# Constants of a delta-rule attention stage: loaded in the stage before, first group summed on VectorE, gate parameters made in the inverse stage

## The chip, the cores and the metric

The kernel runs as one program on one core of a Trainium2 chip. The metric is the time of one execution on the device, in microseconds (us). A line of the profile such as L1421 is that line of the kernel's source. Engines are named PE (TensorE, the matrix products; PEld is its weight load), DVE (VectorE), ACT (ScalarE), POOL (GpSimd) and SP (SyncE, which here issues nearly all transfers). A q behind a name is that engine's instruction queue.

## What is computed

Two transformer layers over 16 sequences of 256 tokens and 128 channels, in float32, each part followed by a residual sum and a layer norm:

```python
x = layernorm(x + L0_attn(x))        # RWKV-like attention with time mixing
x = layernorm(x + L0_ffn(x))         # 8 experts, the best two of each token, relu
x = layernorm(x + L1_attn(x))        # delta rule in chunks of 32 tokens, gate
x = layernorm(x + L1_ffn(x))         # 8 experts, the best one of each token, gelu
```

The change lies in and around the third. Cut to what matters:

```python
q, k, v = silu(conv4(x @ Wq)), silu(conv4(x @ Wk)), silu(conv4(x @ Wv))
beta = sigmoid(x @ Wb)
q, k = l2norm(q), l2norm(k)
A = where(i > j, -(k * beta) @ k.T, 0)      # 32 x 32 for each chunk and head
T = inverse of (I - A), row by row
u, w = T @ (v * beta), T @ (k * beta)
# chunk by chunk: o = q @ S + (q @ k.T, masked) @ (u - w @ S);  S += k.T @ (u - w @ S)
short, long = fir3(v), fir63(v)
logits = (gelu([x, stats(short, long, o, v)] @ gW1 + gb1) @ gW2 + gb2) / exp(log_temp)
floor = 0.05 * sigmoid(floor_param)
p = softmax(logits) * (1 - sum(floor)) + floor
out = p0*short + p1*long + p2*o + p3*v + sigmoid(conv_res_logit)*short + alpha*(x @ Wid)
out = rmsnorm(out) * o_norm_w @ Wo
```

## The kernel before

**Stages.** `block_program` (L2674) builds five stages one after another: the first attention, the experts of two choices (`expert_stage` with tag "b"), `delta_stage` (L2581), `gate_stage` (L1727) and the experts of one choice (tag "d"). `stage` puts an all-engine barrier, the clearing of the stage's semaphores and a second barrier (L2687, L2689) behind each. `delta_stage` is two blocks: `delta_project` (L1227) and `delta_invert` (L1615). Inside a block each engine runs its own program in the order in which it is written; semaphores (`wait_ge`, `then_inc`) are all that orders one engine against another.

**Experts.** Tiles of 128 token rows go through two products, eight tiles deep: SP loads tile j + 8 when the result of tile j is made (`s_y`, L1042, L1043). POOL scatters the results into the rows of `chosen`.

**Projection.** 8 groups of 512 tokens (two sequences). SP loads three parts of a group's rows (L1301: the residual rows and the two chosen expert results), for groups 0 and 1 at once, and then seven tables (L1308). PE, ACT and DVE each begin with `wait_ge(s_w, 112)`, a wait for all seven. POOL sums the parts (`row_sum`, L1412, L1414); DVE takes mean and variance (`row_stats`, L1550, L1553); ACT makes the reciprocal deviation (L1459, L1463); POOL normalises four tiles (`row_norm`, L1421); PE transposes them (L1394 for group 0, L1345 later); ACT copies them to c_xT (L1469); PE projects and convolves (L1350, L1362, L1366). DVE makes the weights by tap c_wc (L1568) ahead of the first `row_stats`. In the loop PE projects group n + 1 while DVE and ACT finish group n.

**Inverse.** PE transposes the chunk matrices A (L1654), ACT copies them (L1687), DVE inverts them row by row (L1712, L1719) while PE computes the long FIR (L1667) from the table keep_toe and ACT copies that out (L1690). Then PE transposes back (L1677) and ACT copies (L1695). SP only stores the FIR rows (L1641).

**Gate.** 8 groups again. SP loads eye32 (L1890), sixteen more tables (L1897), and then for each group the branches (L1877), the rows (L1880) and, from the state, the delta output (L1888). The opening is written out by hand: w_and_u products of groups 0 and 1 (L1942), additions (L1973), transitions (L1957), the transpose of g_wox (L2067), hidden products (L1997), two small products (L2073, L2074), carried products (L1986), then the transposes of the statistics (L2010). ACT makes three parameters (L2338 to L2341), DVE nine small operations (L2422 to L2431), and then the statistics of group 0 (L2445 to L2451), whose squares are ACT's (L2276). From L2524 on runs the loop over groups.

## Time and profile before

| | |
|---|---|
| median of three runs | 1115.13 us (1114.96 to 1118.66) |
| the profiled execution | 1115.36 us, its span 1113.6 us |
| PE busy | 916.2 us, 82% of the span |
| DVE, ACT, POOL busy | 67%, 50%, 41% |
| mean granted clock of PE | 0.89 |
| HBM traffic | 42.69 MB read, 27.51 MB written, 63 GB/s over the span |

The table is one profiled execution, all times in us from the start of the span. The experts of two choices end at about 516, the projection runs from 519 to 667, the inverse to 731, the gate stage from 732.5 to 997, the last experts to the end.
### The profile page before, as it was taken

The numbers are of one execution on the slowest core, as the hardware profiler recorded it, in microseconds if no ns is written. First come the engines' busy times: TensorE is split into PE (matmuls) and PEld (weight loads), VectorE is DVE, ScalarE is ACT, GpSimd is POOL, SyncE is SP. The second block draws the span as 40 slices with busy tenths as digits, with TensorE's granted clock in tenths as the row PEclk, the third lists the DMA queues.
The fourth block names the chain that finished last, engine by engine and source line by source line (L and its number), as shares of the span: only waits on it lengthen the run. The fifth ranks groups of instructions, "written<-read, shape, count | busy, mean of one in ns | idle before, by whom it ended". The sixth has DMA issues, their size and how long they took to land. (4 is left out here: it accounts for less than half of the span.)

```text
span 1113.6 us, 34222 instructions
## 1 busy us (share of the span) xinstructions
PE 916.2 (82%) x12773; PEld 647.2 (58%) x12774; DVE 742.9 (67%) x2240; ACT 556.6 (50%) x1120; POOL 459.1 (41%) x585
## 2 busy tenths in 40 slices
PE   7899999999943999994789969468999987419995
PEld 3466666666622988993344437365565553218884
DVE  3568888898544555552588888903698788745664
ACT  1456667666411554552566753143555554316663
POOL 1001234553373444443477620021135444655776
PEclk7699999999965999997799989766899997758998
DMA  3011112217012222123334231132112234011120
GB/s 90 20 40 49 31 50 59 69 50 227 27 45 65 63 56 60 54 60 101 88 89 87 40 106 57 77 100 64 40 55 65 60 111 139 10 51 49 52 57 17
DMA packets 122117, 73.15 MB, mean 66 GB/s; under 512 B 63363, under 2 KB 108521, under 8 KB 121600
## 3 DMA queue, kind: packets, MB, share of 16 engines
q1 hardware_dynamic: 114176, 58.06, 19.3%
q0 software_dynamic: 6656, 12.70, 3.5%
q8 instruction: 94, 1.54, 0.6%
q10 hardware_dynamic: 1152, 0.53, 0.2%
q14 instruction: 39, 0.32, 0.1%
HBM read 42.69 MB, written 27.51 MB: 63 GB/s over the span
## 5 line engine op out<-in xcount | busy, mean ns | idle before, releaser
L1150 ACT ACTIVATE bx_h<-bx_up,bx_cur 128x128 f32<-128x128 f32 x288 | 82.3, 368 | 98.5 <-PE bx_up L1121 93.8
L593 POOL DMA_INDIRECT regions_b<-a_xo,a_seat x64 | 66.1, 1032 | 128.7 <-DVE a_seat L891 111.7
L1079 POOL DMA_INDIRECT chosen_b<-bx_ys,bx_to x72 | 74.0, 1028 | 92.1 <-DVE bx_ys L1193 69.4
L701 ACT ACTIVATE a_at<-a_scores 128x1024 f32<-128x1024 f32 x64 | 65.7, 1026 | 58.2 <-PE a_scores L463 57.7
L1121 PE MATMUL bx_up<-bx_xT,bx_cur 128*128 128x128 f32 x576 | 82.4, 287 | 2.1 <-DVE bx_cur L1166 0.6
L1103 PE MATMUL bx_down<-bk_w,bx_h 128*128 x576 | 82.1, 285 | 0.3 <-ACT bx_h L1150 0.3
L1121 PEld LDWEIGHTS bx_up<-bx_xT,bx_cur 128*128 128x128 f32 x576 | 71.1, 194 | 11.3 <-DVE bx_cur L1166 5.5
L1103 PEld LDWEIGHTS bx_down<-bk_w,bx_h 128*128 128x128 f32 x576 | 69.7, 191 | 3.5 <-issue 0.5
L1350 PE MATMUL c_bank<-c_xT,c_wc 128*128 128x512 f32 x128 | 62.5, 633 | 7.2 <-DVE keep_attn L1542 6.4
L1166 DVE TENSOR_SCALAR bx_cur<-bk_w 128x516 f32 x72 | 31.3, 434 | 52.9 <-issue 50.4
L458 PE MATMUL a_scores<-a_rk,a_kx 32*128 32x128 f32 (+3 forms) x1024 | 57.7, 290 | 4.6 <-DVE a_kx L769 3.7
L458 PEld LDWEIGHTS a_scores<-a_rk,a_kx 32*128 32x128 f32 x1024 | 43.4, 187 | 29.9 <-issue 14.2
L463 PE MATMUL a_scores<-a_rk,a_kx 32*128 32x32 f32 (+3 forms) x1024 | 53.3, 273 | 0.0
L1421 POOL TENSOR_SCALAR c_xn<-c_part,c_mv,c_rsv 128x128 f32<-128x128 f32 x32 | 35.1, 1107 | 37.0 <-ACT c_rsv L1463 37.0
L2170 POOL COPY g_kak<-keep_k 128x512 f32<-128x512 f32 x16 | 9.8, 616 | 97.3 <-POOLq L2689 67.0
L1350 PEld LDWEIGHTS c_bank<-c_xT,c_wc 128*128 128x128 f32 x128 | 25.6, 204 | 41.5 <-issue 32.6
L1121 PE MATMUL dx_up<-dx_xT,dx_cur 128*128 128x128 f32 x320 | 47.7, 294 | 1.0 <-ACT dx_cur L1139 0.5
L1079 POOL DMA_INDIRECT out_rows<-dx_ys,dx_to x40 | 43.5, 1087 | 8.1 <-issue 8.1
L1150 ACT ACTIVATE dx_h<-dx_up,dx_cur 128x128 f32<-128x128 f32 x160 | 45.1, 363 | 3.2 <-PE dx_up L1121 3.2
L1139 ACT ACTIVATE dx_cur<-space 128x516 f32 x40 | 25.3, 633 | 42.4 <-ACT dx_h L1150 26.6
L1103 PE MATMUL dx_down<-space,dx_h 128*128 x320 | 46.1, 287 | 0.3 <-ACT dx_h L1150 0.3
L1121 PEld LDWEIGHTS dx_up<-dx_xT,dx_cur 128*128 128x128 f32 x320 | 40.4, 198 | 8.7 <-ACT dx_cur L1139 7.4
(440 smaller groups left out, 2462.7 us busy)
## 6 DMA issues: line engine op xcount, KB each, us to landing
bx_xs<-regions_b SPq DMA_DIRECT2D x72, 65.0 KB, 1.8
bk_w<-in_b_w SPq DMA_DIRECT2D x16, 256.0 KB, 6.1
c_part<-chosen_b SPq DMA_DIRECT2D x16, 256.0 KB, 3.8
space<-in_d_w SPq DMA_DIRECT2D x16, 256.0 KB, 5.8
dx_xs<-regions_d SPq DMA_DIRECT2D x40, 65.0 KB, 1.8
a_xp<-in_a_xT SPq DMA_DIRECT2D x8, 256.0 KB, 3.4
a_xr<-in_x SPq DMA_DIRECT2D x8, 256.0 KB
lion_values<-a_vt SPq DMA_DIRECT2D x8, 256.0 KB, 2.7
```

The lines of the kernel that those rows point to most:

```text
L458: mm(S4[:, g, o:o + P - 32 * q], kx[rows, 0, 4 * t + q].rearrange("p h j -> p (h j)"), rk[b][rows, 0, t * P + 32 * q:(t + 1) * P], start=T ...
L463: i = mm(S4[:, g, o + P - 32 * q:o + P + 32], kx[rows, 1, 4 * t + q].rearrange("p h j -> p (h j)"), rk[b][rows, 2, t * P:t * P + 32 * q + 32],
L593: nc.gpsimd.indirect_dma_start(route["regions"], bass.IndirectOffsetOnAxis(ap=seat[b][:, k, t:t + 1], axis=0), xo[b][k][:, t, :], None).th ...
L701: op(at[m % 2][:], S4[:, :, 0:320].rearrange("p g (q k) -> p g q k", q=2)[:, :, :, 0:P], ACT.Copy).then_inc(s_ata, 1)
L1079: nc.gpsimd.indirect_dma_start(dest, bass.IndirectOffsetOnAxis(ap=to[u][:, 0:1], axis=0), ys[u][:], None, bounds_check=dest.shape[0] - 1, ...
L1103: i = mm(BY[u % 2][:, 0:P], h[u % 2][:, f, :], w2[:, bass.ds(e, 1), f, :].rearrange("p e c -> p (e c)"), start=(f == 0), stop=(f == FC - 1))
L1121: i = mm(BU[u % 2][:, f * P:(f + 1) * P], cur[u % 2][:, f * P:(f + 1) * P], xT[u % 2][:], start=True, stop=True)
L1139: op(cur[u % 2][:], w1[:, bass.ds(e, 1), :].rearrange("p e c -> p (e c)"), ACT.Copy).then_inc(s_cur, 1)
L1150: i = op(h[u % 2][:, f, :], BU[u % 2][:, f * P:(f + 1) * P], act_fn, bias=cur[u % 2][:, FC * P + f:FC * P + f + 1])
L1166: v.tensor_scalar(cur[u % 2][:], w1[:, bass.ds(e, 1), :].rearrange("p e c -> p (e c)"), 1.0, None, ALU.mult).then_inc(s_cur, 1)
L1350: i = mm(B[1 + k].rearrange("p (s t) -> p s t", s=GSEQ), wc[:, k, j, :], xT[:, :, j:SEQ + j], start=(j == 0), stop=(j == 3))
L1421: nc.gpsimd.tensor_scalar(xn[:, t, :], part[b][0][:, t, :], mv[:, t, 0:1], rsv[:, t:t + 1], ALU.subtract, ALU.mult).then_inc(s_xn, 1)
```

## The change

Seven tables of the projection are allocated outside the stages and loaded by SP in the experts of two choices, behind the first eight row loads. In the projection the waits for them are gone. The third part of group 0 is issued by ACT, which then loads its table of functions at once. DVE sums and normalises group 0; POOL starts with the sums of group 1 when DVE has made those of group 0. All seventeen tables of the gate stage are loaded by SP at the start of the inverse block, ACT makes the three parameters there after its FIR copies, and in the gate stage DVE makes its parameters ahead of the first transitions, PE transposes g_wox before the first additions, and the hidden products of group 0 stand ahead of the transitions and of the additions of group 1. Some scratch rows of the stage's end lie in g_hid.

```diff
...
             return sem(f"{tag}_{name}")
...
-        s_c = s("identity_in")
...
             sp.dma_start(ident[:], consts[:, columns]).then_inc(s_c, 16)
             for u in range(U):
                 load(u, u)
+            for dst, src in early:
+                sp.dma_start(dst, src).then_inc(s_early, 16)
...
             rounds(sp, body)
+            if early:
+                sp.wait_ge(s_early, 16 * len(early))
...
+def project_tables(nc, ctx, w, consts):
...
+    con = sb("con", [P, columns.stop - columns.start])
+    t = {"C": {k: con[:, a:b] for k, (a, b) in where.items()},
+         "wqkv": sb("wqkv", [P, 3, P]), "wb": sb("wb", [P, P]), "taps": sb("taps", [P, 4]),
+         "tapr": sb("tapr", [P, 2, 4, P]), "fir": sb("fir", [P, 3]), "ident": sb("ident", [P, P])}
+    loads = [(con[:], consts[:, columns]), (t["wqkv"][:], w["wqkv"]), (t["wb"][:], w["wb"]), (t["taps"][:], w["taps"]),
+             (t["ident"][:], consts[:, constant_columns("ident", "ident")[1]]),
+             (t["tapr"][:].rearrange("p k j c -> p (k j c)"), w["tapr"].broadcast_to([P, 8 * P])), (t["fir"][:], w["firs"])]
+    return t, loads
...
+def delta_project(nc, sem, keep, x_parts, xT_out, v_rows, s_rows, tables, w):
...
-            def load(n, b):
-                for k in range(3):
+            def load(n, b, parts=(0, 1, 2)):
+                for k in parts:
                     sp.dma_start(part[b][k][:], one(part_tiles[k], n)).then_inc(s_x[b], 16)
-            load(0, 0)
+            load(0, 0, parts=(0, 1))
             load(1, 1)
-            for dst, src in [(con[:], consts[:, columns]), (wqkv[:], w["wqkv"]), (wb[:], w["wb"]), (taps[:], w["taps"]),
-                             (keep["ident"][:], consts[:, constant_columns("ident", "ident")[1]]),
-                             (tapr[:].rearrange("p k j c -> p (k j c)"), w["tapr"].broadcast_to([P, 8 * P])), (fir[:], w["firs"])]:
-                sp.dma_start(dst, src).then_inc(s_w, 16)
...
         @block.tensor
         def _(pe):
             mm = nc.tensor.matmul
-            pe.wait_ge(s_w, 112)
...
-            row_sum(0, 0, 0)
-            row_norm(0, 0, first=True)
+            pool.wait_ge(s_zs, 2)
             row_sum(1, 1, 0)
             row_norm(1, 1)
             row_sum(2, 0, 1)
...
-            act.wait_ge(s_w, 112)
+            act.dma_start(part[0][2][:], one(part_tiles[2], 0)).then_inc(s_x[0], 16)
+            nc.scalar.preload_act_table_set("natural_log_exp_and_others")
             act.wait_ge(s_set, 5)
...
-            nc.scalar.preload_act_table_set("natural_log_exp_and_others")
             row_logarithm(0)
...
-            dve.wait_ge(s_w, 112)
             dve.wait_ge(s_set, 5)
...
                 i = v.tensor_tensor(wc[:, k], tapr[:, k], wqkv[:, k, :].unsqueeze(1).broadcast_to([P, 4, P]), ALU.mult)
             i.then_inc(s_wc, 1)
             own.restart(dve)
+            x, y0, y1 = part[0]
+            dve.wait_ge(s_x[0], 48)
+            v.tensor_tensor(x[:], x[:], y0[:], ALU.add).then_inc(s_zs, 1)
+            dve.wait_ge(s_zs, 1)
+            v.tensor_tensor(x[:], x[:], y1[:], ALU.add).then_inc(s_zs, 1)
             row_stats(0, 0, first=True)
+            dve.wait_ge(s_rv, 1)
+            for t in range(GT):
+                v.tensor_scalar(xn[:, t, :], x[:, t, :], mv[:, t, 0:1], rsv[:, t:t + 1], ALU.subtract, ALU.mult).then_inc(s_xn, 1)
             row_stats(1, 1)
             convolve_values(0)
...
         def _(sp):
+            for dst, src in loads:
+                sp.dma_start(dst, src).then_inc(s_later, 16)
             sp.wait_ge(s_fc, 8)
...
                    ACT.Copy).then_inc(s_fc, 1)
+            act.wait_ge(s_later, 16 * len(loads))
+            op(later["floor"][:], later["fpar"][:], ACT.Sigmoid)
+            op(later["res"][:], later["crl"][:], ACT.Sigmoid)
+            nc.scalar.preload_act_table_set("natural_log_exp_and_others")
+            op(later["itc"][:], later["temp"][:], ACT.Exp, scale=-1.0)
...
+    loads = [(con[:], consts[:, columns]), (t["eye32"][:], consts[:, constant_columns("eye32", "eye32")[1]]),
+             (t["fpar"][:], w["floor"]), (t["crl"][:], w["crl"]), (t["temp"][:], w["temp"]),
+             (t["g1"][:], w["g1"]), (t["g1s"][:], w["g1s"]), (t["gb1"][:], w["gb1"]), (t["gw2"][:], w["gw2"]),
+             (t["wid"][:], w["wid"]), (t["wox"][:, 0:P], w["wo"]), (t["onw"][:], w["onw"]), (t["gbias"][:], w["gbias"]),
+             (t["alpha"][:], bc(w["alpha"], 4)), (t["gb"][:], bc(route["gate_b"], NE)),
+             (t["ident_gate"][:, P:P + NE], route["gate_w"]),
+             (t["ident_gate"][:, 0:P], consts[:, constant_columns("ident", "ident")[1]])]
+    return t, loads
...
         cnt = sb("cnt", [1, NE])
-        over = sb("over", [1, NE, TOK // P])
+        rows = lambda a, b, n: hid[0:1].rearrange("p j t -> p (j t)")[:, a:b].rearrange("p (k m) -> p k m", k=n)
+        over, le, lt, ef = rows(0, 256, NE), rows(256, 576, NT), rows(576, 896, NT), rows(896, 976, 2)
         base = [sb(f"base{i}", [1, 4 + NE]) for i in range(2)]
         skipped = sb("skipped", [1, NE])
-        le = sb("le", [1, NT, NE])
-        lt = sb("lt", [1, NT, NE])
-        ef = sb("ef", [1, 2, NT])
...
-            sp.dma_start(eye32[:], eye).then_inc(s_in, 16)
-            loads = [(con[:], consts[:, columns]), (g1[:], w["g1"]), (g1s[:], w["g1s"]), (gb1[:], w["gb1"]), (gw2[:], w["gw2"]),
-                     (wid[:], w["wid"]), (wox[:, 0:P], w["wo"]), (onw[:], w["onw"]), (temp[:], w["temp"]), (gbias[:], w["gbias"]),
...
-                sp.dma_start(dst, src).then_inc(s_w, 16)
             for m in range(2):
                 load_branches(m)
...
             w_and_u(0, 0)
             w_and_u(0, 1)
+            pe.wait_ge(s_pv, 1)
+            nc.tensor.transpose(S[:, 0:P], wox[:, 0:P], C["ident"]).then_inc(s_wg, 1)
             additions(0)
             w_and_u(1, 0)
             w_and_u(1, 1)
+            hidden_state(0, 0)
             transition(1, 0)
             transition(1, 1)
-            pe.wait_ge(s_w, NW)
-            pe.wait_ge(s_pv, 1)
-            nc.tensor.transpose(S[:, 0:P], wox[:, 0:P], C["ident"]).then_inc(s_wg, 1)
-            additions(1, 0, 8)
-            hidden_state(0, 0)
-            additions(1, 8, 16)
             hidden_state(0, 1)
+            additions(1)
             pe.wait_ge(s_wgc, 1)
             mm(S[:, P:P + NE], won[:], idx8[:, P:ZC], start=True, stop=True, skip_group_check=True)
             mm(S[:, P + NE:P + 2 * NE], C["ones"], idx8[:, P:ZC], start=True, stop=True, skip_group_check=True).then_inc(s_wg, 1)
...
-            pool.wait_ge(s_w, NW)
...
             copy_wu(0, 0)
             copy_wu(0, 1)
             keep_state(0)
+            act.wait_ge(s_wg, 1)
+            op(won[:], S[:, 0:P], ACT.Copy).then_inc(s_wgc, 1)
             copy_wu(1, 0)
             copy_wu(1, 1)
-            act.wait_ge(s_w, NW)
-            op(floor[:], fpar[:], ACT.Sigmoid).then_inc(s_pa, 1)
-            op(res[:], crl[:], ACT.Sigmoid).then_inc(s_pa, 1)
-            nc.scalar.preload_act_table_set("natural_log_exp_and_others")
-            op(itc[:], temp[:], ACT.Exp, scale=-1.0).then_inc(s_pa, 1)
             act.wait_ge(s_set, 11)
-            act.wait_ge(s_wg, 1)
-            op(won[:], S[:, 0:P], ACT.Copy).then_inc(s_wgc, 1)
             square(0)
             act.wait_ge(s_wg, 2)
             op(wox[:, P:ZC], S[:, P:P + NE], ACT.Copy)
...
-            dve.wait_ge(s_in, 16)
-            transitions(1, 0)
-            transitions(1, 1)
-            dve.wait_ge(s_w, NW)
-            dve.wait_ge(s_set, 11)
-            dve.wait_ge(s_pa, 3)
             own.restart(dve)
-            v.tensor_scalar(pad[:, P:P + 1], C["row"], float(SKIP), None, ALU.add).then_inc(s_padr, 1)
...
             then(v.tensor_scalar(floor[:], floor[:], 0.05, None, ALU.mult))
             then(v.tensor_reduce(keepf[:], floor[:], AX_X, ALU.add))
@@ -2430,6 +2428,10 @@
             then(v.tensor_scalar(g1s[:], g1s[:], C["stat"], None, ALU.mult))
             v.tensor_scalar(wox[:, 0:P], wox[:, 0:P], onw[:, 0:1], float(np.sqrt(32.0)), ALU.mult, ALU.mult).then_inc(s_pv, 1)
             dve.wait_ge(s_pv, 1)
+            transitions(1, 0)
+            transitions(1, 1)
+            dve.wait_ge(s_set, 11)
+            v.tensor_scalar(pad[:, P:P + 1], C["row"], float(SKIP), None, ALU.add).then_inc(s_padr, 1)
...
+    outer = ExitStack()
+    tables, early = project_tables(nc, outer, pick("c"), ins["consts"])
...
         keep, route = expert_tables(nc, ctx, "b", pick("b"), regions, NT_TOP2)
         stage(lion_stage, ins["x"], x1, pick("a"), ins["consts"], route)
-        stage(expert_stage, "b", regions, chosen, route, keep, NT_TOP2, ACT.Relu, ins["consts"], False)
...
```

## Rows read from the trace of the kernel before

**Rows 1.** waits of 515 to 540: us in all, times, longest us.

```profile
PE c_bank L1394 <- POOL c_xn L1421: 22.3, 4, 21.4
```

**Rows 2.** timeline of 500 to 550: start, us, engine, line, what, idle before.

```profile
524.46 1.26 POOL L1412 TENSOR_TENSOR c_part<-c_part 128x512 f32<-128x512 f32 x1 [5.12 <-DMA c_part<-chosen_b]
...
525.80 1.26 POOL L1414 TENSOR_TENSOR c_part<-c_part 128x512 f32<-128x512 f32 x1
...
530.65 1.29 DVE L1568 TENSOR_TENSOR c_wc<-c_tapr,c_wqkv 128x512 f32<-128x512 f32 x2 [16.55 <-DMA c_fir<-in_c_firs]
531.86 0.87 DVE L1550 BATCH_NORM_STATS2 c_bst<-c_part 128x6 f32<-128x128 f32 x4
...
533.82 3.13 POOL L1421 TENSOR_SCALAR c_xn<-c_part,c_mv,c_rsv 128x128 f32<-128x128 f32 x4 [6.75 <-ACT c_rsv L1463]
...
537.51 0.60 ACT L1469 ACTIVATE c_xT<-c_bank 128x512 f32<-128x512 f32 x1 [3.81 <-PE c_bank L1394]
...
538.26 5.06 PE L1350 MATMUL c_bank<-c_xT,c_wc 128*128 128x512 f32 x8 [0.78 <-ACT c_xT L1469]
```

**Rows 3.** two VectorE lines: duration in ns, least/median/most, first and last start.

```profile
L1597 DVE TENSOR_TENSOR c_vb<-c_vs,c_beta x8: 647/650/695, 554.0 to 659.5; 128x512 f32<-128x512 f32 x8
...
L1197 DVE TENSOR_SCALAR dx_ys<-dx_z,dx_mv,dx_rsv x40: 313/316/546, 1012.8 to 1104.6; 128x128 f32<-128x128 f32 x40
```

**Rows 4.** timeline rows of POOL and DVE, and the durations of L1558.

```profile
544.75 1.27 POOL L1412 TENSOR_TENSOR c_part<-c_part 128x512 f32<-128x512 f32 x1
...
544.85 1.46 DVE L1558 TENSOR_SCALAR c_cv<-c_pad,c_taps 128x512 f32<-128x512 f32 x1 [4.00 <-ACT c_pad L1484]
...
L1558 DVE TENSOR_SCALAR c_cv<-c_pad,c_taps x8: 445/702/1458, 544.8 to 651.8; 128x512 f32<-128x512 f32 x8
```

**Rows 5.** the loads of L1301, from issue to landing.

```profile
DMA to landing us min/median/max: 2.9/3.8/4.9
```

**Rows 6.** ACT's timeline at the end of the inverse stage.

```profile
724.13 7.15 ACT L1695 ACTIVATE space<-i_bank 128x512 f32<-128x512 f32 x8 [14.65 <-PE i_bank L1677]
```

**Rows 7.** SP's waits over the span: its reloads in the top-2 experts.

```profile
SPq L1042 <- DVE bx_ys L1193: 57.8, 64, 1.6
```

**Rows 8.** PE's timeline in the opening of the gate stage.

```profile
740.73 0.43 PE L1973 MATMUL g_so<-g_wu,g_kak 32*64 32x32 f32 x6 [1.70 <-issue]
...
742.80 2.38 PE L1942 MATMUL g_identity<-space 32*32 32x64 f32 x64
...
750.75 0.43 PE L1957 MATMUL g_identity<-g_kak,g_wu 32*32 32x64 f32 x7 [3.52 <-issue]
753.89 0.45 PE L2067 MATMUL g_small<-g_con,g_wox 128*128 128x128 f32 x1 [2.71 <-DVE g_wox L2431]
754.27 1.93 PE L1973 MATMUL g_so<-g_wu,g_kak 32*64 32x32 f32 x64
...
766.22 1.11 PE L2010 MATMUL g_small<-g_con,g_stt 128*128 128x128 f32 x4
...
781.30 2.07 PE L1973 MATMUL g_so<-g_wu,g_kak 32*64 32x32 f32 x128
```

**Rows 9.** SP's, ACT's and DVE's timelines in the same opening.

```profile
732.55 0.33 SPq L1890 DMA_DIRECT2D g_eye<-in_consts  x1
...
741.59 0.44 SPq L1897 DMA_DIRECT2D g_ident_gate<-in_consts  x1
...
744.75 2.52 SPq L1888 DMA_DIRECT2D g_X<-g_state  x4
...
754.61 1.90 ACT L2276 ACTIVATE g_xc<-g_X 128x2048 f32<-128x2048 f32 x1
...
756.61 2.29 DVE L2445 TENSOR_REDUCE g_ssq<-g_xc 128x64 f32<-128x2048 f32 x1 [2.87 <-ACT g_xc L2276]
```

**Rows 10.** busy us of PE, PEld, DVE, ACT, POOL, clock, DMA share, GB/s.

```profile
754.00:758.00 4.00, 4.00 (x67) 2.34 (x67) 1.39 (x1) 2.08 (x2) 0.00 (x0) 0.50 0.01 4
...
810.00:860.00 50.00, 46.91 (x1185) 28.99 (x1184) 43.42 (x111) 28.24 (x51) 23.40 (x31) 1.00 0.21 61
```

82 lines of the change are left out of this document (33 added, 49 removed).

## The prediction

> **What bounds the kernel now.** I read the page's busy times first: TensorE (PE) leads them by far, so a gain has to come from stretches in which PE stands still. Next I read the list of waits by stretch around the stage boundaries the diff touches. The longest PE wait near them is in [rows 1]: PE waits 21.4 us for the first normalised rows of the delta stage. Then I read the timeline of that stretch [rows 2]. Its row loads are the first six DMAs on SP, the seven table loads follow, and the first sum on GpSimd (POOL) starts at 524.46. That sum ends at 527.06, but VectorE (DVE) does nothing until 530.65, when the last table, c_fir, is in, because its program begins with a wait for all seven. So the last of two waits is the tables', not the rows'. From 533.82 POOL normalises four tiles, 3.13 us, PE turns them, ScalarE (ACT) copies, and the first projection starts at 538.26. From there PE runs nearly without a break, so that start sets everything up to the end of the stage.
>
> The opening of the gate stage has the same shape [rows 8, 9]. Seventeen loads on SP run from 732.55 to 742.02; PE's transpose of g_wox starts at 753.89, after 2.71 us of waiting for the parameters that DVE makes from them, and only then come the additions of group 1, the hidden products and the carried products, up to the statistics of group 0 at 766.22. Inside it PE also stands still twice with nothing that the profile names: 1.70 us at 739.03 and 3.52 us at 747.23.
>
> **Tables of the projection.** Seven DMAs leave the delta stage and go to SP's queue in the top-2 experts, behind the first eight row loads. At the mean of the gate stage's seventeen, 9.5/17 or 0.56 us each [rows 9], they cost SP 3.9 us. SP there waits for results 64 times, 57.8 us in all [rows 7], and each reload is eight tiles ahead of its use: nothing. If that cover were gone it would be at most these 3.9 us, once. The new final wait of SP is for loads issued 150 us before.
>
> **First group on VectorE.** New chain, one step after the other:
> - Rows in. Before, at 524.46, with the third load issued third on SP; now ACT issues it beside the other two, so the last of the three is issued some 0.5 us sooner. A load took 2.9 to 4.9 us from issue to landing [rows 5]; both queues' loads share the same engines, so the bounds are 523.6 and 525.3. I take 524.0.
> - Two sums on DVE: an operation of this shape takes 0.65 us [rows 3], with its semaphore 0.70, so 1.4 against 2.6 on POOL: 525.4.
> - Statistics of four tiles, then ACT: from 531.86 to 533.82 in [rows 2], 1.96: 527.4. wc, which stood ahead of them, is now made while the rows are under way.
> - Four normalisations on DVE: 0.316 each [rows 3], 1.26 one behind the other and somewhat less where they overlap: 1.1, against 3.13.
> - But POOL sums group 1 in that time. It starts when DVE's second sum is done and group 1's rows are in, 525.7; its two sums, 1.26 each, end at 528.3. In [rows 4] a DVE operation of 512 elements that took 0.445 at least took 1.46 when it began 0.1 us behind a POOL sum of 1.27: it ended only after the sum. So a normalisation that wants to start at 527.4 inside the second sum waits to 528.3; four end at 529.4.
> - From the end of POOL's last normalisation at 536.95 to the projection it is 1.31, the last transpose and ACT's copy among it [rows 2]. So 529.4 and 1.3: 530.7 against 538.26, **7.5 us**. Without the collision 529.8, 8.4 us; with late rows (525.3) 6.2.
>
> What is late next: group 1's rows. Sums end 528.3, statistics on DVE 530.7, ACT 531.3, four normalisations on POOL 534.4. PE wants them behind the whole projection of group 0; its first eight products alone take 5.06 [rows 2], to 535.8, and twelve more follow. That is slack of over 1.4 us, so the steady loop moves as a whole.
>
> The Trainium skill, SBUF — State Buffer, section Who interferes with whom, says that VectorE in certain modes and GpSimd take one port pair in turn, the second to issue standing still for a whole instruction. [rows 4] agree in kind; by the page alone I would have the same 7.5 or, where DVE comes first, 8.4.
>
> **Gate tables moved into the inverse stage.** Seventeen DMAs on SP there, ahead of its wait for the copied FIR rows, which ends at 709.5: 9.5 us as they take now [rows 9], from 668 on, under a cover of over 30. They share the DMA engines with the store of the value rows. ACT stands still for 14.65 us after its last FIR copy, until PE can transpose what DVE has inverted [rows 6], so the FIR products too have that much to spare. ACT gets two sigmoids, an exponential and two table loads behind that last copy; were each as long as the longest ACT row here, 1.90 [rows 9], that is 9.5 us, inside those 14.65. Cost nothing; without cover up to 9.5. The exposed part would be the 32 transposes at the stage's start, which feed DVE: a stall of PE's instructions there would cost its length, 0 to 1.7 [rows 8]. I take 0.
>
> **Opening of the gate stage.** What goes is PE's wait of 2.71, the parameters from DVE's path, and 9.5 us of SP queue ahead of the group 0 rows. PE's own work stays, in another order. With the first stall kept, w_and_u of group 1 still ends at 745.2 [rows 8]. What follows at the lower clock: the two transitions, of 64 products each as the additions' half that took 1.93, so 3.9; then what now runs from 753.89 to 766.22, less the transpose, 11.9. Together 15.8: 761.0. At full clock 128 such products took 2.07 [rows 8], so 15.8 becomes 8.5: 753.7. Beside it DVE: PE has done a hidden product and the transitions by 748.4 (full) or 751.2 (low), DVE's part of them takes 0.8 more, then three reductions of 2.29 and two small steps, 7.2 [rows 9]: 756.5 or 759.2. ACT's squares are in time: the state copies are issued at 742.35 instead of 744.75, land by 747.2 at 2.9 each, and the squares take 1.90 [rows 9]. So the statistics turn at 756.5 (full) to 761.0 (low) instead of 766.22: 5.2 to 9.7 earlier. The granted clock was 0.50 in 754 to 758 [rows 10]. I take the lower clock over three quarters of it, 759.2, and add 1.0 for what is left of the second stall: 760.2, **6.0 us**. With the whole stall of 3.52 and the low clock 764.5, 1.7 us.
>
> About that stall: its place is some 510 instructions after the first, counted in products and weight loads, both with transfers in flight. The Trainium skill, Runtime: NRT & Kernel Launch, section Instruction fetch mechanics, says that instructions arrive in blocks of 256 and that crossing one is mostly hidden; taken literally it gives no second stall here, a gain of 7.0 and a time of 1100.9. The rows show two that aren't hidden; in the new order fewer bytes are in flight at the second.
>
> **Sum.** The profiled execution took 1115.36 us (its span 1113.6 and 1.8 around it, which stay), 0.2 over the median of three, 1115.13. 1115.4 - 7.5 - 6.0 = **1101.9 us**. Moved tables, semaphores and the late-stage scratch rows that now lie in g_hid: 0.
>
> **Rivals.**
> - A, the forecast: 1099.0 to 1104.5, most likely 1101.9. Chance 0.60.
> - B, the gate opening gives its gain back: the lower clock through the whole new order and the full second stall. 1115.4 - 7.5 - 1.7 = 1106.2. For: PE was at 0.50 in 754 to 758 while busy all 4.00 us [rows 10]. Against: the X loads of group 1 now start earlier. 0.17.
> - C, full clock and no stall, no collision on the port: 1115.4 - 8.4 - 9.0 = 1098.0. 0.14.
> - D, the half in the gate stage does nothing: SP, ACT and DVE are freed but additions moved behind a hidden product make the carried chain end where it did, and late rows make the first part 6.2: 1109.2; with a stall of 1.7 in the inverse stage too 1110.9, which counts as no change. 0.07.
> - E, slower: the clock. A shift by 13.5 us puts the gate loop under other decisions on the clock. Its stretch 810 to 860 is at 1.00 with PE busy 46.91 of 50 [rows 10], so work there takes twice its time at the other level. The point from which it decides is 13.5/0.94, some 14.4 us of now-full-clock PE work running at 1.2 GHz; 20 us would give 1115.4 - 13.5 + 18.8 = 1120.7. For it: 0.50 in [rows 10] in spite of a busy PE. Against: the loop holds 1.00 today for whole groups. 0.02.
>
> **Range and chances.** 1097.8 to 1107.8 holds A, B and C; D and E, 0.09, and the outer ends of the others are left out. 0.5% is 5.6 us, about what a measurement of this kernel can tell from no change: faster is below 1109.5. A, B, C and most of D give 0.94; same 0.04; slower 0.02.
>
> **What would show it.** Right: PE's first product L1350 (by its new number) some 12 us after the stage's first load instead of 19.2; DVE's wc before the rows land; a first DVE normalisation stretched by the end of a POOL sum; the same time as before between that product and the last FIR copy; in the gate stage no PE wait for g_wox, and the statistics' transposes 27 to 28 us after the stage's first load instead of 33.7. Wrong: rows of group 0 landing after 526; POOL's normalisation of group 1 ending after PE wants it; a new PE gap in the inverse stage's first 4 us; a wait for g_stt behind 762; or granted clock 0.50 in the gate loop where it was 1.00.

## The result, and the profile after

The changed kernel took **1101.01 us** in the median (1099.11 to 1102.58, 4 runs), the kernel before 1115.05 in the same comparison (1110.4 to 1118.66, 4 runs): ratio 0.9863, 95% interval 0.9832 to 0.9894. The forecast was 1101.9 us, with a range of 1097.8 to 1107.8. The profiled execution of the changed kernel took 1099.11 us, its span is 1097.1; that of before 1115.36, span 1113.6. Medians and ratios in this document leave out the slow executions, those at a lower granted clock or over 1.5% above the fastest of their kernel (one of the changed kernel took 1174.4 us at a mean clock of 0.71). The page, with TensorE's busy time and the granted clock in 40 slices:

```profile
span 1097.1 us, 34218 instructions
...
PE 909.6 (83%) x12773; PEld 645.9 (59%) x12774; DVE 747.3 (68%) x2246; ACT 556.6 (51%) x1120; POOL 453.0 (41%) x579
...
PEclk8899999999965999998799989868999997758998
```

The opening of the delta stage, which answers to [rows 2] (timeline: start, us, engine, line, what, idle before and who ended it):

```profile
514.49 0.39 SPq L1315 DMA_DIRECT2D c_part<-rows  x1
514.50 0.46 ACTq L1462 DMA_DIRECT2D c_part<-chosen_b  x1
514.76 1.29 DVE L1575 TENSOR_TENSOR c_wc<-c_tapr,c_wqkv 128x512 f32<-128x512 f32 x2 [5.27 <-POOL c_vs L1416]
...
519.82 0.69 DVE L1580 TENSOR_TENSOR c_part<-c_part 128x512 f32<-128x512 f32 x1 [3.77 <-DMA c_part<-chosen_b]
...
521.27 0.87 DVE L1557 BATCH_NORM_STATS2 c_bst<-c_part 128x6 f32<-128x128 f32 x4
...
522.47 1.26 POOL L1421 TENSOR_TENSOR c_part<-c_part 128x512 f32<-128x512 f32 x1 [7.75 <-DMA c_part<-chosen_b]
...
523.23 2.43 DVE L1586 TENSOR_SCALAR c_xn<-c_part,c_mv,c_rsv 128x128 f32<-128x128 f32 x4 [0.67 <-ACT c_rsv L1472]
523.81 1.26 POOL L1423 TENSOR_TENSOR c_part<-c_part 128x512 f32<-128x512 f32 x1
...
525.21 0.99 PE L1403 MATMUL c_bank<-c_con,c_xn 128*128 128x128 f32 x3 [0.86 <-DVE c_xn L1586]
...
526.97 6.29 PE L1359 MATMUL c_bank<-c_xT,c_wc 128*128 128x512 f32 x8 [0.78 <-ACT c_xT L1478]
```

Read it against [rows 2] from the top. The stage begins at 514.5 instead of 519.1. The projection's table (L1575) is written in the first 1.6 us and no longer stands ahead of the statistics, so the chain is rows, sums, statistics, normalisation, with nothing between them. The first projection product comes 12.47 us after the stage's first instruction instead of 19.15. Two things in it are new. The two POOL sums of group 1 lie over the four normalisations, which take 2.43 us where the forecast had 2.0 (1.1 of their own and 0.9 of waiting). And the first eight products take 6.29 us where [rows 2] had 5.06.

The opening of the gate stage, TensorE's timeline, which answers to [rows 8]:

```profile
724.45 1.93 PE L1955 MATMUL g_wu_xy<-space 32*32 32x64 f32 x64 [3.58 <-PEq L2691]
...
728.50 0.47 PE L2074 MATMUL g_small<-g_con,g_wox 128*128 128x128 f32 x1
729.31 3.88 PE L1986 MATMUL g_so<-g_wu,g_kak 32*64 32x32 f32 x128 [0.34 <-issue]
...
740.49 0.38 PE L1970 MATMUL g_identity<-g_kak,g_wu 32*32 32x64 f32 x10 [0.45 <-issue]
...
744.98 0.42 PE L1986 MATMUL g_so<-g_wu,g_kak 32*64 32x32 f32 x13 [1.20 <-issue]
...
748.93 0.74 PE L1999 MATMUL g_so<-g_state,g_xyx 32*64 32x32 f32 x18 [0.96 <-issue]
749.61 1.11 PE L2023 MATMUL g_small<-g_con,g_stt 128*128 128x128 f32 x4
```

The transpose of g_wox is the third thing TensorE does, with no wait for parameters. The stalls of 1.70 and 3.52 us in [rows 8] have become 0.45, 1.20 and 0.96. The statistics are turned at 749.61, 25.16 us after the stage's first product; in the kernel before it was 33.62. The granted clock of this stretch (columns as in [rows 10]):

```profile
732.00:736.00 4.00, 4.00 (x145) 3.94 (x144) 0.00 (x0) 1.85 (x4) 1.72 (x3) 0.50 0.08 20
736.00:740.00 4.00, 3.86 (x150) 2.69 (x141) 0.59 (x2) 2.15 (x2) 0.00 (x0) 0.87 0.61 169
740.00:744.00 4.00, 3.33 (x130) 2.34 (x127) 3.25 (x6) 0.36 (x1) 0.80 (x2) 1.00 0.49 151
744.00:748.00 4.00, 2.98 (x127) 2.79 (x127) 4.00 (x2) 0.80 (x4) 1.73 (x3) 0.91 0.02 4
748.00:752.00 4.00, 3.07 (x74) 2.67 (x77) 0.74 (x3) 1.64 (x3) 0.00 (x0) 0.50 0.02 6
```

The transitions, the hidden products and the second additions run at the full level, where the prediction had priced three quarters of them at the lower one. Behind the statistics the clock is at 0.50 again.

**Where the time went.** I measured every execution at the same marks. "Experts", "delta" and "gate" are the starts of the top-2 experts, the delta stage and the gate stage's first product. From the delta stage's start: its first projection product (with what eight took), the value projection, and the first of the 32 transposes that open the inverse stage (with what all took). From the gate stage's first product: statistics turned, and the first logits on VectorE. All us.

| execution | span | experts | delta | first product (8) | values | transposes (32) | their end to gate | statistics | logits |
|---|---|---|---|---|---|---|---|---|---|
| before | 1113.6 | 349.6 | 519.1 | 19.15 (5.06) | 24.05 | 148.86 (3.83) | 60.80 | 33.62 | 47.86 |
| changed | 1097.1 | 344.4 | 514.5 | 12.47 (6.29) | 18.60 | 143.21 (5.78) | 60.97 | 25.16 | 41.02 |
| after_again | 1103.0 | 349.3 | 519.4 | 12.18 (6.52) | 18.54 | 143.20 (5.87) | 60.92 | 25.16 | 41.10 |
| project_only | 1110.5 | 348.1 | 517.6 | 12.43 (6.62) | 18.89 | 143.55 (5.91) | 61.21 | 31.95 | 47.78 |
| gate_only | 1108.2 | 349.2 | 519.3 | 19.69 (6.21) | 25.74 | 150.41 (5.71) | 60.69 | 24.86 | 40.97 |
| no_collision | 1098.7 | 349.1 | 519.2 | 10.80 (5.46) | 16.09 | 140.69 (5.39) | 61.01 | 25.39 | 39.62 |
| third_on_sp | 1151.0 | 390.4 | 565.3 | 12.90 (5.49) | 18.23 | 142.84 (5.40) | 61.01 | 24.84 | 40.62 |
| pool_group0 | 1145.5 | 384.3 | 558.2 | 14.52 (5.26) | 19.62 | 144.25 (5.28) | 60.69 | 25.12 | 40.86 |
| gate_order | 1150.6 | 389.9 | 565.1 | 12.34 (5.66) | 17.84 | 142.62 (5.38) | 61.02 | 25.03 | 40.72 |
| warm | 1147.6 | 386.2 | 560.6 | 12.50 (3.67) | 16.01 | 144.38 (3.83) | 61.14 | 24.66 | 40.82 |
| no_collision_2 | 1096.4 | 346.9 | 517.0 | 10.80 (5.44) | 16.08 | 140.69 (5.38) | 61.26 | 24.11 | 40.13 |
| warm_fit | 1093.6 | 346.9 | 516.8 | 10.76 (5.37) | 15.97 | 139.54 (3.84) | 61.10 | 24.51 | 40.21 |
| warm_all | 1094.7 | 347.4 | 518.3 | 11.16 (3.67) | 14.67 | 138.76 (3.83) | 60.70 | 24.05 | 41.25 |

The first two rows account for the 16.5 us between the profiled spans. 4.6 lie ahead of the delta stage: 5.2 ahead of the top-2 experts, in code that the change doesn't touch, and 0.6 given back in them. 3.5 come from the delta and inverse stages together (19.15 - 12.47 = 6.7 at the first product, 5.65 at the inverse's start, 3.7 behind its 32 transposes, 3.5 at the gate stage). 6.8 come from the gate stage's opening (8.5 at the statistics, 6.8 at the logits). 1.5 are scattered behind that. So of the gain in this pair only 10.4 us lie where the change is; the delta half is worth half of what I forecast, and a part of it is lost again at the inverse stage's start, in work that the change left alone. First before, then after (TensorE's timelines):

```profile
663.20 3.63 PE L1386 MATMUL c_bank<-c_kq,c_kn 32*32 32x64 f32 x128 [7.14 <-DVE c_kq L1602]
667.96 3.83 PE L1654 MATMUL i_bank<-keep_ident,space 128*128 128x128 f32 x32 [1.13 <-PEq L1239]
```

```profile
652.93 3.63 PE L1395 MATMUL c_bank<-c_kq,c_kn 32*32 32x64 f32 x128 [7.12 <-DVE c_kq L1617]
657.70 5.78 PE L1671 MATMUL i_bank<-c_ident,space 128*128 128x128 f32 x32 [1.14 <-PEq L1259]
```

The gaps ahead of both are the same to 0.02 us; only the duration of the transposes differs, 3.83 against 5.78. That, the slower first products, and the 4.6 us ahead of the delta stage were the questions for the runs.

### The profile page after: what moved, and what is told of

Same layout as the page of the kernel before. It is cut to its first block and busy times, and to the rows that moved or that the text cites. A ratio compares the mean times of both kernels' runs of the same rounds, so it can differ in the third digit from the quotient of the medians.

```text
span 1097.1 us, 34218 instructions
## 1 busy us (share of the span) xinstructions
PE 909.6 (83%) x12773; PEld 645.9 (59%) x12774; DVE 747.3 (68%) x2246; ACT 556.6 (51%) x1120; POOL 453.0 (41%) x579
## 3 DMA queue, kind: packets, MB, share of 16 engines
q1 hardware_dynamic: 113648, 57.80, 19.7%
## 5 line engine op out<-in xcount | busy, mean ns | idle before, releaser
L458 PE MATMUL a_scores<-a_rk,a_kx 32*128 32x128 f32 (+3 forms) x1024 | 57.7, 291 | 5.1 <-DVE a_kx L769 4.1
L458 PEld LDWEIGHTS a_scores<-a_rk,a_kx 32*128 32x128 f32 x1024 | 43.5, 187 | 29.6 <-DVE a_at L909 14.2
L1430 POOL TENSOR_SCALAR c_xn<-c_part,c_mv,c_rsv 128x128 f32<-128x128 f32 x28 | 31.9, 1149 | 31.8 <-ACT c_rsv L1472 31.8
```

Of the source, the lines that this page charges most:

```text
L458: mm(S4[:, g, o:o + P - 32 * q], kx[rows, 0, 4 * t + q].rearrange("p h j -> p (h j)"), rk[b][rows, 0, t * P + 32 * q:(t + 1) * P], start=T ...
L1430: nc.gpsimd.tensor_scalar(xn[:, t, :], part[b][0][:, t, :], mv[:, t, 0:1], rsv[:, t:t + 1], ALU.subtract, ALU.mult).then_inc(s_xn, 1)
```

## The experiments

Theory: the two halves of the change act where I said, independently; what the delta half lost against the sum it lost to POOL's sums, which hold up VectorE's normalisations, and to a low granted clock behind TensorE's idle times. Rivals: the halves interact; ACT's queue, the sums on VectorE or the order in the gate stage are what brings the gain; the longer durations come from the code and not from the clock.

**The changed kernel again**, no edit.

> The changed kernel once more, beside the halves. Theory (two independent gains, the rest is noise of one execution): 13.5 to 14.5 us under the kernel before; in its profile the first projection product again 12.5 us behind the stage's first load, the first projection of the values (which follows eight products) 18.6 behind it, the statistics' transposes of the gate stage 25.2 behind its first product. Rival (the profiled pair, 16.5 us apart, shows the true gain, and the first attention's part of it is real): 16 us or more, and the top-2 experts start at 344 again instead of 349.6.

Measured: 1102.89 us in the median of three executions (1096.9 to 1105.04), before 1114.75, ratio 0.9878 (0.9823 to 0.9933). That is 11.9 us by the medians and 13.6 by the ratio, whose interval spans 7.5 to 19.7. Its experts begin at 349.3, not at 344.4, and all marks behind the delta stage's start are within 0.3 us of the first execution's. So most of the 4.6 us ahead of the delta stage belong to the execution and not to the change. With equal starts the spans differ by 10.6 us (1113.6 - 1103.0).

**The delta half alone**: the gate's tables are loaded and its parameters made in the gate stage again, in the old order.

```
 inverse, sp:   -for dst, src in loads: sp.dma_start(dst, src).then_inc(s_later, 16)
 inverse, act:  -op(later["floor"]...), op(later["res"]...), op(later["itc"]...)
 gate, sp:      +for dst, src in [loads[0]] + loads[2:]: sp.dma_start(dst, src).then_inc(s_w, 16)
 gate, pe:      transpose of wox, additions(1, 0, 8), hidden_state(0, 0), additions(1, 8, 16) as before
```

> Only the first half of the change: projection tables in the top-2 experts, third load on ACT, group 0 on VectorE; the gate stage as before. Theory (the halves add up): 5.5 to 7 us under the kernel before, the part kept after the slower clock at the first products; the gate stage's statistics are turned 33 to 34 us after its first product. Rival (the halves interfere, so that one brings most): 2 us or 10 us.

Measured: 1110.22 us, 4.5 under before, ratio 0.9955 (0.9935 to 0.9976). The first product is at +12.43 as in the changed kernel, and the gate stage behaves as before: 2.67 us of stall, then 2.72 of wait for g_wox.

```profile
744.77 0.43 PE L1968 MATMUL g_identity<-g_kak,g_wu 32*32 32x64 f32 x7 [2.67 <-issue]
747.92 0.45 PE L2078 MATMUL g_small<-g_con,g_wox 128*128 128x128 f32 x1 [2.72 <-DVE g_wox L2442]
```

**The gate half alone**: tables of the projection loaded in the delta stage and waited for, group 0 summed and normalised by POOL.

```
 project, sp:   +for dst, src in w_loads: sp.dma_start(dst, src).then_inc(s_w, 16)
 project, dve:  +dve.wait_ge(s_w, 112)      -the two sums and four normalisations of group 0
 project, pool: +row_sum(0, 0, 0)           +row_norm(0, 0, first=True)
```

> Only the second half: gate tables and parameters in the inverse stage and the new order of PE; the projection's opening as before, with the tables loaded behind the rows and waited for. Theory: 6.8 to 8 us under the kernel before, the statistics' transposes 25 us after the gate stage's first product, the first projection product 19.2 us behind the first load. Rival (the gain in the gate stage is given back in the loop by a lower clock): 4 us or less.

Measured: 1109.06 us, 5.7 under before, ratio 0.9946 (0.992 to 0.9971); statistics at +24.86, logits at +40.97, 6.9 us sooner than before. The two halves bring 4.5 and 5.7, together 10.2 by the medians and 11.0 by the ratios, the whole 11.9 and 13.6 in the same comparison, on three executions. The intervals are too wide to tell a sum from an interaction of a few us. The marks are sharper: each half moves its own marks as the whole does (first product at +12.43 alone and +12.18 and +12.47 in the whole, logits at +40.97 and +41.0 to 41.1) and leaves the other's about where they were, so no interaction is seen. Both halves came out about 1 us under the range that I expected. This run has the old code up to the inverse stage, and yet its first eight products take 6.21 us and its 32 transposes 5.71:

```profile
664.94 3.64 PE L1399 MATMUL c_bank<-c_kq,c_kn 32*32 32x64 f32 x128 [7.13 <-DVE c_kq L1615]
669.71 5.71 PE L1669 MATMUL i_bank<-c_ident,space 128*128 128x128 f32 x32 [1.13 <-PEq L1259]
```

So the longer durations are not brought by the new code. The granted clock says what they are (columns as in [rows 10]; the first two rows are of the kernel before, the others of this run):

```profile
664.00:668.00 4.00, 2.87 (x109) 2.66 (x100) 2.37 (x6) 0.00 (x0) 1.54 (x3) 0.58 1.02 403
668.00:672.00 4.00, 4.00 (x40) 3.82 (x44) 0.00 (x0) 3.31 (x7) 0.00 (x0) 1.00 0.92 393
...
668.00:672.00 4.00, 2.87 (x34) 2.66 (x27) 0.76 (x2) 0.91 (x2) 0.00 (x0) 0.50 1.01 423
672.00:676.00 4.00, 4.00 (x39) 3.70 (x41) 0.00 (x0) 3.36 (x7) 0.00 (x0) 0.77 0.86 251
```

By these rows the clock came back to 1.00 at 667.4 in the kernel before, 0.6 us ahead of the transposes, and here at 673.8, 4.1 us behind their start; counted from the last scores' first product that is 4.2 and 8.9 us, after the same gaps. The first eight products fit too: they take 3.67 us at 1.00 (the run with idle products, below), so 5.06 has 2.8 us at 0.50 in it and 6.21 has 5.1. The profiled execution of before had been lucky twice; what brings the clock back sooner in one execution than in another stays open. Measured against this run instead, the delta half is worth 6.8 us at the gate stage's start (150.41 + 5.71 + 60.69 against 143.21 + 5.78 + 60.97), against the other 3.5.

**Without the collision**: POOL begins group 1's sums only when VectorE has normalised group 0.

```
-            pool.wait_ge(s_zs, 2)
+            pool.wait_ge(s_xn, 4)
```

> The changed kernel, but POOL starts the sums of group 1 only when DVE has normalised group 0 (one wait on another semaphore). Theory (port collision): DVE's four normalisations take 1.1 us together instead of 2.43, the first projection product comes 11.2 us behind the first load instead of 12.5, and the whole is 1 to 1.3 us faster than the changed kernel, because group 1's rows have slack. Rival (the first normalisation is long for another reason, such as its wait for the deviation): 2.4 us again and no difference.

Measured: 1100.8 us, 2.1 under the changed kernel's median in the same comparison, but the ratio to before, 0.9887 (0.9852 to 0.9923), is no better than the changed kernel's 0.9878: the times don't show a gain. The marks do.

```profile
527.60 1.12 DVE L1586 TENSOR_SCALAR c_xn<-c_part,c_mv,c_rsv 128x128 f32<-128x128 f32 x4 [0.67 <-ACT c_rsv L1472]
528.00 1.25 PE L1403 MATMUL c_bank<-c_con,c_xn 128*128 128x128 f32 x4 [14.83 <-DVE c_xn L1586]
528.80 1.26 POOL L1421 TENSOR_TENSOR c_part<-c_part 128x512 f32<-128x512 f32 x1 [9.34 <-DVE c_xn L1586]
...
530.03 5.46 PE L1359 MATMUL c_bank<-c_xT,c_wc 128*128 128x512 f32 x8 [0.78 <-ACT c_xT L1478]
```

The four normalisations take 1.12 us, the 1.1 of the prediction, instead of 2.43 to 2.53. The collision is shown, and its price is 1.3 to 1.4 us: the first product comes at +10.80. The end of the 32 transposes came at +146.1 in both executions without the collision and at +148.0 to +149.5 in the five with it (the changed kernel twice, the delta half alone, and two of the runs below). The value projection comes 2.45 us sooner, 16.09 against 18.54, more than the collision, because the eight products behind it took 5.46 instead of 6.52. POOL's later start costs nothing that can be seen.

**The third load back on SP**:

```
-            act.dma_start(part[0][2][:], one(part_tiles[2], 0)).then_inc(s_x[0], 16)     (ACT)
+            load(0, 0)                          instead of load(0, 0, parts=(0, 1))      (SP)
```

> The kernel after the change, with the third load of the first group's rows issued from SP's queue behind the other two, as in the kernel before, instead of from ACT's. The kernel before had its rows 5.36 us after the stage's first instruction, the changed one 5.33 us. Theory: ACT's queue brings nothing. Rows in at +5.3 to +5.4 us, first product of the projection at +12.2 to +12.5 us, time the same as the changed kernel's within 0.3 us. Rival (the prediction's step): three loads behind one another on SP cost 0.5 us, so rows at +5.8, first product at +12.8 to +13.0, and 0.5 us more in all.

Measured: 1150.79 us, before 1163.55 on this chip, ratio 0.9871 (0.9791 to 0.9951). The chip of this comparison spends some 40 us more ahead of the top-2 experts (below), in every kernel, so only the marks behind it are compared. Rows at +5.90, first product at +12.90; two others on this chip with ACT's load had the rows at +5.12 and +4.81, and one more with all three loads on SP at +5.44. My expectation was wrong and the rival is right here. Over all executions, with all three loads on SP the rows came at 5.35, 5.43, 5.90 and 6.58, with one of them on ACT at 4.81, 4.93, 4.96, 4.97, 5.08, 5.12, 5.25, 5.32 and 5.48: medians 5.67 and 5.08. The 0.5 us of the prediction are there in the medians, but with four executions on one side, of different kernels and chips, and ranges that overlap, that is likely and not shown. The recorded pair had the least of the one and nearly the most of the other. Its time can't be told apart from that of the others.

**Tables early, group 0 on POOL**: the edit before, and sums and normalisations of group 0 on POOL.

> The kernel after the change, but the first group's rows are summed and normalised by POOL and its third load is on SP, as before; the projection's constants are still loaded and its table built in the expert stage. It separates the two halves of the projection's change. Theory: the early table lets the statistics start as soon as POOL's two sums (1.26 us each, from +5.3) end at +8.0, statistics and ACT's root 2.0, POOL's normalisation 3.1, ACT's copy and the transposes 1.3 to 1.5: first product at +14.6 us, 2.3 us later than in the changed kernel (+12.2 to 12.5) and 4.6 us sooner than before (+19.15); the time 2 to 2.5 us over the changed kernel's. Rival: the sums on VectorE are what brings it, and the first product stays at +18 to +19 us.

Measured: 1151.99 us (before 1163.55, ratio 0.9897, 0.9821 to 0.9974).

```profile
563.61 1.26 POOL L1421 TENSOR_TENSOR c_part<-c_part 128x512 f32<-128x512 f32 x1 [5.21 <-DMA c_part<-chosen_b]
...
566.24 0.87 DVE L1557 BATCH_NORM_STATS2 c_bst<-c_part 128x6 f32<-128x128 f32 x4 [6.51 <-POOL c_part L1423]
...
568.27 3.12 POOL L1430 TENSOR_SCALAR c_xn<-c_part,c_mv,c_rsv 128x128 f32<-128x128 f32 x4 [2.06 <-ACT c_rsv L1472]
```

The first product is at +14.52, as expected (+14.6). So of the 6.7 us at the first product the early tables bring 4.6 (19.15 - 14.52) and the work on VectorE, with the third load on ACT, 2.0 to 2.3; with that load on SP it is 1.6 (against 12.90), its rows having come 0.5 us later. The rival, by which the tables would bring nothing, falls.

**The old order in the gate stage**, with tables and parameters early:

```
 gate, pe:  w_and_u(0), additions(0), w_and_u(1), transition(1, 0), transition(1, 1),
            transpose of wox, additions(1, 0, 8), hidden_state(0, 0), additions(1, 8, 16), hidden_state(0, 1), ...
```

> The kernel after the change, but TensorE's and ACT's order at the opening of the gate stage is that of the kernel before (the transpose of g_wox and its copy behind the transitions, half of the second additions ahead of the first hidden state); tables and parameters are still prepared in the inverse stage. Theory: what brought the time is that no table or parameter is built at the opening any more; the order alone is worth at most 1 us: statistics turned 25.2 to 26.2 us after the stage's first product (changed kernel 25.2, before 33.6), first output of the gate's large sums at +41 to +42. Rival: the order carried half of the gain, statistics at +28 to +30 us and the time 3 us or more over the changed kernel's.

Measured: 1150.29 us (ratio 0.9893, 0.9795 to 0.9991); statistics at +25.03, logits at +40.72, against 25.16 and 41.02. So the order of TensorE and ACT is worth nothing that can be seen, and the gain of the gate half comes from what no longer stands in the opening. Which part of that brings it, the loads or the parameters, no run separates; VectorE's new order was kept here as well. TensorE has stalls of 1.25 and 1.41 us here, in its own places.

**Idle products for the clock, too many**: without the collision, and with products nobody uses, on a free bank: four behind the rows' arrival, fourteen ahead of the last scores.

```
+            pe.wait_ge(s_x[0], 48)
+            for _ in range(4):  mm(B[7], wqkv[:, 0, :], tapr..., start=True, stop=True)
             (ahead of the first transposes; 14 of the same ahead of the last group's scores)
```

> The kernel without the collision (POOL's sum of the second group waits for VectorE's four normalisations), and with products on TensorE whose result nobody uses: 4 of 512 columns between the arrival of the rows and the first transposes, 14 of them ahead of the last group's scores, where TensorE stood idle for 7.1 us. Theory: the work after these two gaps is slow only because the granted clock has fallen to 0.50 in them. Then the first eight projection products take 3.6 to 4.5 us instead of 5.46, the last scores 2.0 instead of 3.64, the 32 transposes at the inverse's start 3.8 instead of 5.4, in sum 4 to 5 us under the kernel without the collision (span 1098.7, so about 1094). Rival: these durations come from the operands or the code and not from the clock, or the clock falls all the same; then the time is as without the collision, or up to 1 us longer where the idle products hold TensorE.

Measured: 1148.45 us in the median of four executions, before 1163.55, ratio 0.985 (0.9768 to 0.9931).

```profile
565.45 6.46 PE L1405 MATMUL c_bank<-c_tapr,c_wqkv 128*128 128x512 f32 x8 [10.88 <-DMA c_part<-chosen_b]
...
573.12 3.67 PE L1359 MATMUL c_bank<-c_xT,c_wc 128*128 128x512 f32 x8 [0.78 <-ACT c_xT L1483]
...
689.65 12.28 PE L1390 MATMUL c_bank<-c_tapr,c_wqkv 128*128 128x512 f32 x28 [0.19 <-DVE keep_attn L1554]
701.86 1.99 PE L1397 MATMUL c_bank<-c_kq,c_kn 32*32 32x64 f32 x128
704.99 3.83 PE L1676 MATMUL i_bank<-c_ident,space 128*128 128x128 f32 x32 [1.14 <-PEq L1259]
```

All three durations came as the theory of the clock has them: 3.67, 1.99 and 3.83 us instead of 5.46, 3.64 and 5.39. The same instructions on the same operands take up to half as long when TensorE was busy in the gap ahead of them. But one such product is two passes of 0.44 us at the full clock, and four of them at the lower one took 6.46, 14 took 12.28 in a gap of 7.1, so what they won they gave away as a delay: the 32 transposes ended at +148.2, against +146.1 without idle products.

**Idle products that fit.** The kernel without the collision once more as the measure, and the same with four idle products as soon as VectorE has written the projection's table and seven ahead of the last scores.

> The kernel without the collision once more, beside the two that follow, as their measure. By the earlier execution: rows in at +5.0, first product of the projection at +10.8, value projection at +16.1, the inverse's first transposes at +140.7 us after the stage's first instruction, the last scores 3.64 and the 32 transposes 5.3 us; from the 32 transposes' end to the first product of the gate stage 61 us. The time 3 to 4 us under the changed kernel's.

> The kernel without the collision, with idle products on TensorE that fit into its gaps: in the run before, four of them after the rows' arrival took 6.46 us and held the first transposes, and fourteen ahead of the last scores took 12.28 us in a gap of 7.1. Here the four begin as soon as VectorE has written the projection's table (+1.5), and end at +8.0, ahead of the first transposes at +8.4; seven of 0.88 us stand ahead of the last scores. Theory (the clock): first product at +10.2 to +10.8, value projection at +14.0 to +14.6 instead of +16.1, last scores 2.0 instead of 3.64, the 32 transposes 3.8 instead of 5.3: 4.5 to 5 us under the kernel without the collision. Rival: a clock held up here is taken back by the throttle in the work that follows, so that the stage's end comes less than 2 us sooner.

```
-            pe.wait_ge(s_x[0], 48)      +            pe.wait_ge(s_wc, 1)
-            range(14 if last else 0)    +            range(7 if last else 0)
```

Measured: 1099.65 us without idle products (1098.45 to 1102.11, ratio to before 0.9869, 0.984 to 0.9899) and **1095.44 with them** (1093.02 to 1097.24, ratio 0.9825, 0.9794 to 0.9855): 4.2 us, with ranges that don't touch. The profile shows 2.7 of it at the end of the 32 transposes (140.69 + 5.38 against 139.54 + 3.84).

```profile
518.39 5.09 PE L1405 MATMUL c_bank<-c_tapr,c_wqkv 128*128 128x512 f32 x8 [7.64 <-DVE c_wc L1580]
525.66 1.10 PE L1408 MATMUL c_bank<-c_con,c_xn 128*128 128x128 f32 x4 [2.18 <-DVE c_xn L1591]
527.54 5.37 PE L1359 MATMUL c_bank<-c_xT,c_wc 128*128 128x512 f32 x8 [0.78 <-ACT c_xT L1483]
...
647.07 6.17 PE L1390 MATMUL c_bank<-c_tapr,c_wqkv 128*128 128x512 f32 x14
653.17 1.99 PE L1397 MATMUL c_bank<-c_kq,c_kn 32*32 32x64 f32 x128
656.31 3.84 PE L1676 MATMUL i_bank<-c_ident,space 128*128 128x128 f32 x32 [1.14 <-PEq L1259]
```

The seven worked. The four at the start didn't: behind them TensorE stood still for 2.18 us, and the first products took 5.37 as without them. The clock did come up under the idle products, but it was not kept:

```profile
524.00:528.00 4.00, 1.56 (x5) 0.85 (x6) 1.68 (x9) 1.10 (x3) 1.46 (x2) 1.00 0.01 2
528.00:532.00 4.00, 4.00 (x7) 1.64 (x6) 1.25 (x8) 1.53 (x3) 2.00 (x3) 0.57 0.71 168
```

Half of my expectation failed there.

**Idle products in the inverse stage too**: five from the 23rd step of VectorE's inversion on, two behind the back-transposes.

```
+            pe.wait_ge(s_dve, 92)
+            for _ in range(5):  mm(R[0], C["ident"], V..., start=True, stop=True)      (ahead of the back-transposes; 2 behind them)
```

> As the one before, and besides five idle products in the inverse stage from the 23rd step of VectorE's inversion (some 8.5 us before the 32 back-transposes), and two behind the back-transposes, where TensorE stands idle for 3.6 us up to the gate stage. Theory: the back-transposes take 4.3 to 5 us instead of 6.1 (ACT's eight copies, 0.6 us each, bound them), the first two products groups of the gate stage 2.2 us instead of 4.1 together and the first additions 1.95 instead of 3.88, so that the statistics are turned 21 to 22 us after the stage's first product instead of 25.4: 4 to 5 us under the kernel before it. Rival: statistics wait for DMAs, ACT and the hidden state, and the gate gains under 1.5 us; or the clock falls sooner in the stretch that follows (it fell at 750 us in the changed kernel and products there took 2 us more), and the gate's first large sums come at +39 all the same.

Measured: 1093.66 us (1088.84 to 1096.7), ratio 0.9803 (0.9771 to 0.9835), the fastest kernel of the study; its runs overlap with those of the one before, so whether the additional products bring anything is open. In the delta stage the four at the start did work this time, with a gap of 1.77 us behind them: 3.67 us for the first eight. In the gate stage the rival that the gain stays under 1.5 us holds:

```profile
725.35 3.71 PE L1997 MATMUL g_so<-g_wu,g_kak 32*64 32x32 f32 x128 [0.21 <-issue]
...
742.11 3.64 PE L2010 MATMUL g_so<-g_state,g_xyx 32*64 32x32 f32 x128
```

The first additions still took 3.71, and the carried products ran at the lower clock, 3.64; in the changed kernel they have 2.83 us of work. They took 3.64 in three runs without idle products in the inverse stage too, so this can't be laid to them. Logits at +41.25, not sooner than +40.13 without. In the back-transposes TensorE now waits for ACT's copies four by four, so that little is won up to the gate stage: 60.70 against 61.10.

## Why the prediction was right

The time was forecast to 0.9 us. The mechanisms stood, but two terms were off against each other and the profiled pair added what belongs to neither.

- **Rows in**, 0.5 us sooner through ACT's queue: nothing in the recorded pair (5.33 after, 5.36 before), about 0.6 in the medians of all executions. The term is likely and not shown.
- **Two sums on VectorE** 1.4, **statistics and ACT** 1.96, **last normalisation to first product** 1.3: measured 1.45, 1.96 (521.27 to 523.23) and 1.31.
- **The collision**: seen rightly from [rows 4], priced too low. I let POOL's second sum hold one normalisation for 0.9 us. Group 1's rows came later than I had put them, 8.0 us after the stage's start instead of 6.6. So both sums lay over the normalisations, each held one of them, and the longest took 1.42 us: 2.43 in all, 1.3 more than the 1.12 without POOL. The Trainium skill, SBUF — State Buffer, section Who interferes with whom, has VectorE and GpSimd take their shared port pair in turn; the run without the collision agrees, 1.12 against 2.43.
- **Late is next**: right. POOL's normalisation of group 1 ends long before TensorE wants it, and the steady loop moved as a whole: from the first product to the inverse's first transposes 130.7 us after, 129.7 before. The 1.0 more goes with the first eight products, which took 1.2 more at the lower clock.
- **Sum of the delta half, 7.5**: measured 6.7 at the first product, 3.5 at the gate stage in the recorded pair, 6.8 against the execution of the old code in the run with the gate half alone; 4.5 in the median of the delta half alone. The term that failed is one I hadn't written: that the work right behind TensorE's idle times runs at a granted clock that differs between executions, here by 1.2 us in the first products and 1.9 in the 32 transposes. I had taken 5.06 and 3.83 from one execution as if they were fixed.
- **Tables moved, cost nothing**: right in all parts. SP's loads in the experts don't show in the marks (the experts took 169.5 and 170.1 us in two executions without them, 169.5 to 170.9 in seven with them, those of the chip with the longer times left out), ACT's sigmoids, exponential and two table loads take 701.20 to 704.3, ahead of an idle time of 11.37 us which was 14.65 in [rows 6], and from the transposes' end to the gate stage it is 60.8 us before and 61.0 after. The 32 transposes had no stall.
- **Gate opening, 6.0**: 8.5 at the statistics, 6.8 at the logits. The statistics came at +25.2 where I had +27.6. The reason is the clock, 0.87 and 1.00 from 736 to 744 where I took the lower level for three quarters. The stalls were sized rightly in sum: 2.6 us of them against 5.2 in [rows 8], and I had left 2.7, the first one whole and 1.0 of the second. But two of the three that came lay in places where I had none. Then w_and_u of group 2 and the hidden statistics at 0.50 took back 1.6 us by the logits. 5.7 in the median of the gate half alone. That this term came near its forecast owes something to luck: the clock gave more than I had taken, and then took a part of it back.
- **The stalls**: those of before, in stages that load tables at their opening, are 1.70, 3.52 and (delta half alone) 2.67 us; in the openings without these loads they are 0.2 to 1.82. The rule of the Trainium skill, Runtime: NRT & Kernel Launch, section Instruction fetch mechanics, that crossing a block is mostly hidden, would have given 7.0 for this half and fits 6.8 better than my 6.0. It isn't borne out in kind, since three stalls are left in the changed kernel. Counted in products and weight loads from the stage's first, TensorE's unexplained gaps above 0.3 us lie behind the 499th, 1009th, 1263rd or 1517th in all executions without idle products (and one of 0.3 to 0.8 us behind some 256). With idle products, which put 72, 44 and 72 more of these instructions ahead of the stage, they lie behind the 1193rd, the 1221st and 1475th, and the 1191st: 70, 42 and 72 sooner. So they belong to places of the program, 254 or twice 255 instructions apart, and not to a wait that the kernel states; the one behind some 256 didn't move. Behind the 1009th they took 3.52 and 2.67 us with the loads, and without them 0.45 to 1.25, or nothing. That the loads make them longer is a correlation; no run changed the loads alone.
- **The rivals**: E is out, the stretch 810 to 860 is at 1.00 with TensorE busy 46.03 us, against 46.91 in [rows 10]. B's way back showed itself in small, 1.6 us. C's full clock and missing collision each came true in part, the first without help, the second by an edit.
- **What carried the time to 1101**: against an execution of the old code with the slower durations, the delta half moves the marks by 6.8 us and the gate half by 6.9 at the logits, 13.7 in all where I had 7.5 and 6.0. The first comparison shows 14.0 between the medians (15.3 by its ratio), the second 11.9 (13.6 by its ratio, with three executions), the halves alone 10.2 to 11.0 in sum. The forecast of 13.5 lies within the intervals of both comparisons (0.9832 to 0.9894 and 0.9823 to 0.9933). That it met the median to 0.9 us is partly luck: the delta half came out under its term and the gate half over it, and one comparison can't place the time to better than some 3.5 us.

## What to carry to other kernels

A stage's opening is bound by what its slowest engine waits for last: look whether that is a table that an earlier stage could have loaded, and only then at which engine does the work. When work moves to another engine, look also at what its old engine does instead in the same microseconds, and make that wait if the two hold each other up: one changed wait brought the first product 1.4 us sooner here, at no cost that can be seen. Before a term is read off one execution, ask whether the row stands right behind an idle time of TensorE; if so, look up its granted clock: its duration can differ by half between executions of the same code (3.83 and 5.78 us here). Idle products that fit the gap can bring the shorter one; seven ahead of the last scores did so both times, four at the start once of two.
